# The top's complex measuring product by three real products instead of four

## What is computed

```
mr = sup_r @ meas_Mr.T - sup_i @ meas_Mi.T
mi = sup_r @ meas_Mi.T + sup_i @ meas_Mr.T
amp = sqrt(mr ** 2 + mi ** 2)
z = gelu(layernorm(amp @ post_W.T + post_b))
h = relu([z, r_x] @ W_top1 + b_top1)
y = relu(h @ W_top2 + b_top2) @ W_top3
```

## Time and profile before

| | |
|---|---|
| Time, median of 3 runs | 2832.51 us (2831.17 to 2833.8) |
| The profiled execution: time | 2832.54 us |
| The profiled execution: span of the trace | 2830.7 us |
| TensorE, matmul | busy 2720.3 us, 96% |
| VectorE | busy 2091.1 us, 74% |
| ScalarE | busy 1235.7 us, 44% |
| GpSimd | busy 152.6 us, 5% |
| Mean granted TensorE clock | 0.983 of full |

### The profile page before, as it was taken

How to read it: one execution, slowest core, us unless ns; L and a number is a source line. 1 busy time by engine, 2 the same in 40 slices (tenths; PEclk the granted TensorE clock), 3 DMA queues, 4 the chain that set the end, 5 groups by cost and what they waited for, 6 DMA issues and landing times. The chain is left out here.

```text
span 2830.7 us, 43833 instructions
## 1 busy us (share of the span) xinstructions
PE 2720.3 (96%) x16320; PEld 2339.1 (83%) x16320; DVE 2091.1 (74%) x3548; ACT 1235.7 (44%) x1873; POOL 152.6 (5%) x185
## 2 busy tenths in 40 slices
PE   8999999999899998999999999999999899999797
PEld 6888888888778876888889999999999777877686
DVE  5697778873567865687877877877777769999863
ACT  2222442244543336333454554444444556464643
POOL 2000000000000000010100100100000000000200
PEclk9999999999999999999999999999999899999899
DMA  6555556544755867468723223232232654445310
GB/s 244 202 187 185 187 192 220 193 160 152 240 169 185 266 233 267 135 207 287 250 81 105 60 89 89 60 97 81 69 101 68 169 129 96 104 96 133 104 34 12
DMA packets 493716, 420.41 MB, mean 149 GB/s; under 512 B 282273, under 2 KB 397089, under 8 KB 493345
## 3 DMA queue, kind: packets, MB, share of 16 engines
q1 hardware_dynamic: 459168, 341.20, 39.4%
q0 software_dynamic: 17792, 60.89, 5.7%
q10 hardware_dynamic: 16640, 16.78, 1.8%
HBM read 328.62 MB, written 90.18 MB: 148 GB/s over the span
## 5 line engine op out<-in xcount | busy, mean ns | idle before, releaser
L54 PE MATMUL banks<-a_hi 128*128 128x512 f32 x1024 | 399.8, 390 | 14.0 <-DVE a_lo L367 13.9
L55 PE MATMUL banks<-a_lo,a_hi 128*128 128x512 f32 x1024 | 399.2, 390 | 0.0
L56 PE MATMUL banks<-a_hi,a_lo 128*128 128x512 f32 x1024 | 399.1, 390 | 0.0
L54 PE MATMUL banks<-b_hi 128*128 128x512 f32 x896 | 355.8, 397 | 22.6 <-DVE b_lo L790 11.9
L55 PE MATMUL banks<-b_lo,b_hi 128*128 128x512 f32 x896 | 352.0, 393 | 0.0
L56 PE MATMUL banks<-b_hi,b_lo 128*128 128x512 f32 x896 | 351.7, 393 | 0.0
L54 PE MATMUL banks<-sx,g_hi 128*128 128x256 f32 x1024 | 294.4, 287 | 5.8 <-DMA sx<-s_scr 4.0
L55 PE MATMUL banks<-sx,g_hi 128*128 128x256 f32 x1024 | 291.4, 285 | 0.0
L56 PE MATMUL banks<-sx,g_lo 128*128 128x256 f32 x1024 | 291.3, 284 | 0.0
L1639 DVE TENSOR_SCALAR t_ks<-banks,cols 64x256 f32<-64x256 f32 x512 | 236.5, 482 | 28.9 <-PE banks L56 22.1
L54 PEld LDWEIGHTS banks<-a_hi 128*128 128x128 f32 x1024 | 192.7, 188 | 55.5 <-DVE a_lo L367 14.8
(11 more groups left out here) (202 smaller groups left out, 5517.5 us busy)
## 6 DMA issues: line engine op xcount, KB each, us to landing
w_ring<-w_first SPq DMA_DIRECT2D x192, 512.0 KB, 4.3
w_ring<-w_second SPq DMA_DIRECT2D x160, 512.0 KB, 5.0
sx<-s_scr SPq DMA_DIRECT2D x64, 512.0 KB, 4.4
a_scr<-t_at SPq DMA_DIRECT2D x256, 128.0 KB, 2.1
s_axng<-a_scr SPq DMA_DIRECT2D x64, 512.0 KB, 5.2
g_wraw<-w_pieces SPq DMA_DIRECT2D x74, 256.0 KB, 4.7
w_ring<-w_second SPq DMA_DIRECT2D x64, 256.0 KB, 5.3
c<-h_scr ACTq DMA_DIRECT2D x16, 1024.0 KB, 7.8
```

What stands on the lines that cost most here:

```text
L54: mm(out, ahi, bhi, start=first, stop=False, **more)
L55: mm(out, ahi, blo, start=False, stop=False, **more)
L56: return mm(out, alo, bhi, start=False, stop=last, **more)
```

## The change

With P1 = sr Mr, P2 = si Mi and P3 = (sr + si)(Mr + Mi), the two parts are mr = P1 - P2 and mi = P3 - P1 - P2.

- **TensorE**: `measure(t, x)` with x = 0, 1, 2 makes one product of 12 matmuls each, into banks 2, 3 and 4; measure(e, 0) and measure(e, 1) stand before the transposes, measure(e, 2) after them. The banks of post, top_one and top_two move up by one. Each product waits for its own weights' rest only.
- **Weights**: VectorE adds Mr and Mi (`weights_summed`, 2048 columns in one operation), and makes the rests of Mr, Mi and the sum (`m_rests`, three operations of 2048). ScalarE makes the high part of the sum (`sum_high`). GpSimd makes no rests. ScalarE's eight pieces are done before negate(LAST, 3).
- **States**: the negated part is gone. ScalarE copies si out of its bank (`sup_copy`), VectorE adds sr (`sup_sum`), and the sum is split as the third part.
- **Parts**: ScalarE copies P1 out of its bank (`m_copy`), VectorE makes mr, P1 + P2 and mi in three operations (`m_parts`), ScalarE squares both parts in one operation.
- **Order**: pair (0,1) comes after unit vector 3; sum_m(0) before pair (0,3); pair (1,3) is in step 2, pair (2,3) and the product in step 3; the statistics of the layer norm come before sum_m. `length` and `scale` of the last tile end step 4. SyncE's waits before the later pieces are for the high parts, and its last store comes after two loads.

```diff
+    W_MS = 27
...
-        B_SUP, B_M, B_POST, B_TOP1, B_TOP2 = 0, 2, 4, 5, 6
+        B_SUP, B_M, B_POST, B_TOP1, B_TOP2 = 0, 2, 5, 6, 7
...
                 if 2 * NP <= i - TR < 2 * NP + M_RESTS:
-                    sp.wait_ge(m_split, i - TR - 2 * NP + 1)
+                    sp.wait_ge(w_hi, i - TR + 1)
...
-            store(LAST)
             sup_back(6)
             top_x(3)
+            store(LAST)
...
-            for i in range(2 * NP, 2 * NP + M_RESTS):
-                pool.wait_ge(w_hi, i + 1)
-                pool.tensor_tensor(wlo[:, i % NP, :], wraw[:, i % NP, :], f32(whi[:, i % NP, :]), ALU.subtract).then_inc(m_split, 1)
...
-            def sup_high(t):
-                for x, sign in ((0, 1), (1, 1), (1, -1)):
-                    act.wait_ge(s_turned, t * 2 + x + 1)
+            def sup_copy(t):
+                act.wait_ge(s_turned, t * 2 + 2)
+                if t >= 1:
...
+                act.activation(s_sum, g.ps[:, B_SUP + 1, :], ACT.Copy).then_inc(s_copied, 1)
+
+            def m_copy(t):
+                act.wait_ge(measured, t * 3 + 1)
...
+                act.activation(m_sum, g.ps[:, B_M, :], ACT.Copy).then_inc(m_copied, 1)
+
+            def sup_high(t, xs=range(3)):
+                for x in xs:
+                    if x < 2:
+                        act.wait_ge(s_turned, t * 2 + x + 1)
+                    else:
+                        act.wait_ge(s_summed, t + 1)
                     if t >= 2:
-                        act.wait_ge(measured, 2 * (t - 1))
-                    hi = turned(t, x if sign > 0 else 2)[0]
-                    act.activation(hi, g.ps[:, B_SUP + x, :], ACT.Copy, scale=float(sign)).then_inc(s_hi, 1)
...
-            def square_m(t, part):
-                act.wait_ge(measured, 2 * t + part + 1)
...
-                act.activation(sqm[:, part, :], g.ps[:, B_M + part, :], ACT.Square).then_inc(m_squared, 1)
+                        act.wait_ge(measured, 3 * (t - 1))
+                    src = g.ps[:, B_SUP + x, :] if x < 2 else s_sum
+                    act.activation(turned(t, x)[0], src, ACT.Copy).then_inc(s_hi, 1)
...
+            def sum_high():
+                act.wait_ge(ms_made, 1)
+                act.activation(whi[:, W_MS:W_MS + KD, :], wraw[:, W_MS:W_MS + KD, :], ACT.Copy).then_inc(ms_hi, 1)
+
+            def square_m(t):
+                act.wait_ge(m_step, 3 * t + 3)
+                act.activation(sqm, sqm, ACT.Square).then_inc(m_squared, 1)
...
             squares(t, 0)
+            pieces(2 * NP, 2 * NP + 2 * KD)
             negate(t, 3)
             squares(t, 1)
             lengths(t, 0)
-            pieces(2 * NP, 2 * NP + KD)
             squares(t, 2)
-            pieces(2 * NP + KD, 2 * NP + 2 * KD)
+            sum_high()
             squares(t, 3)
-            sup_high(0)
+            sup_high(0, (0, 1))
             lengths(t, 1)
             strengths(t)
+            sup_copy(0)
+            m_copy(0)
+            sup_high(0, (2,))
+            sup_high(1, (0,))
+            sup_copy(1)
+            sup_high(1, (1,))
             begin(t, 0, 1)
+            sup_high(1, (2,))
             length(t - 1)
-            square_m(0, 0)
+            square_m(0)
+            amplitude(0)
+            pieces(2 * NP + 2 * KD, 2 * NP + 3 * KD)
             begin(t, 0, 2)
             scale(t - 1)
-            sup_high(1)
             begin(t, 0, 3)
-            pieces(2 * NP + 2 * KD, 2 * NP + 3 * KD)
-            square_m(0, 1)
-            amplitude(0)
             for e in range(1, TT + 3):
-                if e == 4:
-                    length(LAST)
                 if e < TT:
-                    square_m(e, 0)
+                    m_copy(e)
                 if e + 1 < TT:
-                    sup_high(e + 1)
+                    sup_high(e + 1, (0,))
+                    sup_copy(e + 1)
+                    sup_high(e + 1, (1, 2))
                 if e - 1 < TT:
                     amp_high(e - 1)
                 if 0 <= e - 2 < TT:
@@ -1621,12 +1652,15 @@
                 if e == 1:
                     pieces(2 * NP + 3 * KD, 2 * NP + N_TOP)
                 if e == 4:
-                    scale(LAST)
+                    length(LAST)
                 if e < TT:
-                    square_m(e, 1)
-                    amplitude(e)
+                    square_m(e)
                 if e - 1 < TT:
                     deviation(e - 1)
+                if e < TT:
+                    amplitude(e)
+                if e == 4:
+                    scale(LAST)
...
-            def sup_low(t):
-                for x, sign in ((0, 1), (1, 1), (1, -1)):
-                    hi, lo = turned(t, x if sign > 0 else 2)
-                    dve.wait_ge(s_hi, t * 3 + (1 if x == 0 else 3))
-                    if sign > 0:
-                        ins = dve.tensor_tensor(lo, g.ps[:, B_SUP + x, :], f32(hi), ALU.subtract)
-                    else:
-                        ins = dve.scalar_tensor_tensor(out=lo, in0=g.ps[:, B_SUP + x, :], scalar=-1.0, in1=f32(hi),
-                                                       op0=ALU.mult, op1=ALU.subtract)
-                    ins.then_inc(s_split, 1)
...
+            def weights_summed():
...
+                dve.wait_ge(multiplied, LAST * 8 + 8)
+                dve.tensor_tensor(wraw[:, W_MS:W_MS + KD, :], wraw[:, W_MR:W_MR + KD, :], wraw[:, W_MI:W_MI + KD, :],
+                                  ALU.add).then_inc(ms_made, 1)
+
+            def m_rests(w):
...
+                    dve.wait_ge(ms_made, 1)
+                dve.tensor_tensor(wlo[:, w:w + KD, :], wraw[:, w:w + KD, :], f32(whi[:, w:w + KD, :]),
+                                  ALU.subtract).then_inc(m_split, 1)
+
+            def sup_sum(t):
+                dve.wait_ge(s_hi, t * 3 + 1)
+                dve.wait_ge(s_copied, t + 1)
+                dve.tensor_tensor(s_sum, g.ps[:, B_SUP, :], s_sum, ALU.add).then_inc(s_summed, 1)
+
+            def sup_low(t, xs=range(3)):
+                for x in xs:
+                    hi, lo = turned(t, x)
+                    dve.wait_ge(s_hi, t * 3 + x + 1)
+                    dve.tensor_tensor(lo, g.ps[:, B_SUP + x, :] if x < 2 else s_sum, f32(hi), ALU.subtract).then_inc(s_split, 1)
+
+            def m_parts(t):
+                dve.wait_ge(m_copied, t + 1)
+                dve.wait_ge(measured, t * 3 + 2)
+                dve.tensor_tensor(sqm[:, 0, :], m_sum, g.ps[:, B_M + 1, :], ALU.subtract).then_inc(m_step, 1)
+                dve.tensor_tensor(m_sum, m_sum, g.ps[:, B_M + 1, :], ALU.add).then_inc(m_step, 1)
+                dve.wait_ge(m_step, t * 3 + 2)
+                dve.wait_ge(measured, t * 3 + 3)
+                dve.tensor_tensor(sqm[:, 1, :], g.ps[:, B_M + 2, :], m_sum, ALU.subtract).then_inc(m_step, 1)
 
             def sum_m(t):
-                dve.wait_ge(m_squared, t * 2 + 2)
+                dve.wait_ge(m_squared, t + 1)
                 if t >= 1:
                     dve.wait_ge(a_turned, t)
...
-            tile.units()
-            sup_low(0)
-            tile.pair(0, 1)
+            tile.refine(0)
+            tile.unit_vector(0)
+            tile.unit_vector(1)
+            weights_summed()
+            m_rests(W_MR)
+            tile.add_squares(1)
+            sup_low(0, (0, 1))
+            m_rests(W_MI)
             tile.refine(1)
             tile.unit_vector(2)
+            sup_sum(0)
+            m_rests(W_MS)
+            sup_low(0, (2,))
             tile.unit_vector(3)
+            tile.pair(0, 1)
+            sup_low(1, (0,))
+            sup_sum(1)
+            sup_low(1, (1,))
+            m_parts(0)
+            sup_low(1, (2,))
             tile.pairs_02()
             inverse_length(LAST - 1)
-            sup_low(1)
+            sum_m(0)
             tile.pairs_03()
             pieces(2 * NP + 2 * KD, 2 * NP + 3 * KD)
-            sum_m(0)
             dve.wait_ge(row_in, 16)
             for e in range(1, TT + 3):
-                if e == 4:
-                    inverse_length(LAST)
                 if e + 1 < TT:
-                    sup_low(e + 1)
+                    sup_low(e + 1, (0,))
+                    sup_sum(e + 1)
+                    sup_low(e + 1, (1, 2))
...
+                if e < TT:
+                    m_parts(e)
                 if e == 1:
                     pieces(2 * NP + 3 * KD, 2 * NP + N_TOP)
                     tile.pairs_12()
-                if e == 2:
-                    tile.pairs_23()
+                if e - 1 < TT:
+                    statistics(e - 1)
                 if e < TT:
                     sum_m(e)
                 if e - 1 < TT:
@@ -2015,10 +2091,13 @@
                     add_rx(e - 2)
                 if 0 <= e - 3 < TT:
                     output(e - 3)
-                if e == 1:
+                if e == 2:
                     tile.pairs_13()
-                if e == 2:
+                if e == 3:
+                    tile.pairs_23()
                     tile.product()
+                if e == 4:
```

(83 more changed lines are left out.)

## The result

The changed kernel takes 2835.65 us (median of 20 runs, 2831.01 to 2840.87), the kernel before 2831.09 beside it (20 runs): ratio 1.0020, 95% interval 1.0014 to 1.0026. Two of the 20 runs of the kernel before were slow ones, 3040.91 and 4537.28 us, and are left out of the ratio. The changed kernel is slower by 4.6 us in medians, with 96 matmuls fewer. The profiled execution took 2834.71 us, its span is 2832.9.

What follows compares the result with a forecast made beforehand. VectorE was taken to bound the ramp, TensorE the steady steps. Step 5's transposes at 2756.1, two steps of 17.3 to 2790.7, plus 11.2 and 34.2, 1.84 outside the span and 0.5 give 2838.5 us; range 2831 to 2845.

Steps and rivals of the forecast that it cites:

- the walk: Stretch-by-stretch sum of times from the ramp's head to the end of the span, forecast 2838.5 us; chance 0.62.
- Steady steps: Top's loop once TensorE bounds it: 12 matmuls fewer take a step from 20.03 to 17.3 us.
- the z rival: Steady steps: z chain takes over, 2842.5 us at 1 us delay, upper end 2846 if TensorE's clock falls; chance 0.16.
- Head: Ramp's start on VectorE, from second unit vector to step 1: VectorE enters step 1 some 8.1 us late.
- The wait for begin: Ramp's head: VectorE's pair (0,3) waits for ScalarE's begin(0,2) behind amplitude(0) and four pieces, 3.3 us.
- Steps 1 to 3: VectorE in the first passes of the top's loop: 16.5, 19.0 and 26.7 us, ending at 2739.0.
- TensorE's gaps: Ramp: TensorE stands some 10 us before post(0) and 8.7 before post(3), waiting for VectorE.
- T(5): Start of TensorE's transposes in step 5 of the top's loop: forecast 2756.1, 13.4 us late.
- the slow matmuls: After the gap before post(3): 8 to 9 matmuls at 1.2 GHz, 1.6 us, charged once.
- End: Start of step 7's transposes to step 8's 11.2 us, then 34.2 to the end of the span.
- the 0.5 for releases: A dozen releases between engines on the path, 0.03 to 0.1 us each: 0.5 us added to the sum.
- TensorE is the bound everywhere: Whole span: the ramp gives the removed matmuls back too, 2808 to 2820, say 2814 us; chance 0.12.

Runs made afterwards that it cites:

- a2: Changed kernel with the high and low part of the sum of states moved behind gelu and z's low part; 2828.97 us, ratio 0.9995 to the kernel before.
- a1: Changed kernel with ScalarE's begin(0,2) ahead of amplitude(0) and four pieces; 2832.47 us, ratio 0.9999 to the kernel before.
- a0: Changed kernel run again with no edit, for repeatability; 2836.24 us, ratio 1.0016 to the kernel before.
- a3: Changed kernel with the product of the sums made twice, so as many matmuls as before; 2843.74 us, ratio 1.0045 to the kernel before.
- b4: Changed kernel with the edits of a1, a2 and b1 together; 2828.33 us, ratio 0.9989 to the kernel before.
- c2: b4 with the pair's four operations before z's low part and its weights at the end of the step; 2826.43 us, ratio 0.9984 to the kernel before.
- b3: Kernel before with its measuring rests on VectorE, ScalarE's eight pieces before negate(3) and SyncE waiting for high parts; 2828.83 us, ratio 0.9989 to the kernel before.
- c1: Changed kernel with only the edits of a1 and a2; 2829.80 us, ratio 0.9991 to the kernel before.
- b2: Changed kernel with the rests of Mr and Mi back on GpSimd, the sum's rest on VectorE; 2838.02 us, ratio 1.0022 to the kernel before.
- b1: Changed kernel with VectorE's pairs (1,3) and (2,3) moved into the wait for z's high part; 2835.25 us, ratio 1.0006 to the kernel before.
- c4: Changed kernel with pair (1,3) back in step 1, pair (2,3) and product in step 2, plus a1 and a2; 2828.55 us, ratio 0.9991.

## Why the prediction was right

The forecast was 2838.5, 6.0 above the profiled execution of before; measured were 2835.65, 4.6 above before in medians, 5.7 by the ratio (4.0 to 7.4). The ratio lies on the 0.2% at which the chances of "slower" and "within" were parted, so it decides for neither of the two. Counted from the mark, the walk gave 207.9 us to the end of the span, the trace has 207.4 (before 202.0). That this execution is 3.8 us below 2838.5 is mostly its earlier start of the mark, 3.1 us, which no term was about.

- **Steady steps**: forecast 17.3, measured 17.8. This is where the walk erred and the z rival was right in kind: TensorE waits 0.22 and 0.29 us for z's low part, and a2 brings 17.3 back. Its upper end did not come: such gaps, repeated each step, left the matmuls at 0.23 us, 2.4 GHz. The waits that the cited section of the Trainium skill, "HAM oscillation — how this bites in real kernels", tells of are several microseconds long, so the prediction was wrong to take the upper end as likely by it, and this trace does not speak against it.
- **Head**: step 1 began at 46.5, forecast 48.0: the sum's high part takes 1.91 us, not 2.2, and VectorE waited 0.55 before the last squares instead of 1.25. That is 0.6 of the 1.5; the rest is durations rounded up. The wait for begin was 3.25, forecast 3.3, and a1 shows its price at the end to be 3.3. ScalarE's eight pieces cost nothing, as said: it still waits 4.80 us there for the DMA.
- **Steps 1 to 3**: 17.3, 17.9 and 26.8 against 16.5, 19.0 and 26.7; the fold ended at 108.6, forecast 110.3. The waits for z were 2.67 and 2.67, taken as 2.7. The wait for ScalarE's copies, 1.01, stands at the end of step 1, where the walk had it in step 2, and step 3 has none: its "same waits 3.1" are only those for z and the deviation.
- **TensorE's gaps**: 7.80 before post(0), 9.41 in a0 (some 10), and 8.92 before post(3) (8.7). From post(3) to T(5) 14.0, forecast 13.9. Charging the slow matmuls once was right.
- **End**: T(7) to T(8) 11.23, forecast 11.2; from there 34.1, forecast 34.2. The trace is 1.1 us later than the walk in the steps and 1.1 earlier at T(5). That these cancel is luck, and the 0.5 for releases is what is left over: the mechanism was right to 1 to 2 us a stretch, not to the 0.5 us of the sum.
- **The rival "TensorE is the bound everywhere"** fell. a3 prices the 96 matmuls at 7.5 us; up to T(5) they are worth 0.7. The advice cited there to improve the busiest engine first stands one section earlier in that page of the Trainium skill, "Identifying the Most-Contended Engine", and that section does not go by TensorE's busy share.

What the walk didn't see is that its loss does not come with three products as such. Begin behind the pieces (3.3), the sum's parts ahead of z (3.0) and the pairs' place (3.4) are order alone; with all three put right (b4) T(8) goes from 173.3 to 163.2, 4.6 us before the kernel before's, and the time to 0.9989 of it (0.9984 in c2, with half the pair). But b3 keeps four products and is at 0.9989. The intervals overlap, so these runs don't show that three products are worth more than four here. Open are also b3 with orders of its own, which wasn't tried, and an order that leaves no gap before post(3).

## What to carry to other kernels

Price removed work where the engine that did it is the last to arrive. In a ramp that another engine fills it was worth next to nothing here (0.7 us of the matmuls up to T(5)), while a wait of the filling engine came out whole at the end (3.25 us, 3.3 at T(8)). Then look at the order around new work: a wait of 3 us on the filling engine, and parts put ahead of a chain that has just lost its slack, were the whole loss at T(8) (c1). Work taken off an engine that then waits is no gain (b2). Fill a wait only with work that fits into it, and judge a move by its neighbours too: the pairs' move gave 0.4 us at T(8) alone and 3.4 once begin and z's chain had been put right.

## What was unexpected of the hardware

The length of a gap does not say whether TensorE comes back slow. After 2.96 us (b1) 13 matmuls ran at 0.43 us from the start; after 3.98 us (c4) four ran at 0.23 and only then about eight at 0.39 to 0.43; after 2.36 us (b4) none was slow. The rows of c4:

```profile
2689.82 0.47 PE L54 MATMUL banks<-g_hi 128*128 128x512 f32 x1 [3.98 <-DVE g_lo L1976]
...
2690.59 0.39 PE L54 MATMUL banks<-g_hi 128*128 128x512 f32 x1
2690.82 0.59 PE L55 MATMUL banks<-g_lo,g_hi 128*128 128x512 f32 x1
2691.21 0.63 PE L56 MATMUL banks<-g_hi,g_lo 128*128 128x512 f32 x1
```

What decides it these runs don't settle. Where it came in these profiles, 3 to 14 matmuls were slow, 0.2 us each: 0.6 to 2.8 us a gap, up to as much as the waits that the orders were made to save.
